# Layer norm of the next tile pair ahead of the last tile's output tail

## The reference

```python
x = x + attention(layernorm(x))     # local window + pooled latents, gated
h = layernorm(x)                    # second phase starts here
for blk in range(3):
    y = qlora_linear(h, 2*blk)      # dequantized 1024x1024 + rank-32 LoRA + bias
    y = gelu(layernorm(y))
    h = qlora_linear(y, 2*blk + 1) + h
x = x + h
```

## Time and profile before

| | us |
|---|---|
| median of 2 runs | 3964.92 (3957.31 to 3972.54) |
| profiled execution, its own time | 3984.25 |
| its span, core 2, the slowest | 3982.6 |
| other cores | 3947.6 to 3982.0 |

### The profile page before, as it was taken

The page is one execution under the profiler, slowest core; times in us unless marked ns, Lnnn a source line. Parts: engine busy times, 40 slices in busy tenths (PEclk is TensorE's granted clock), DMA queues, the critical chain, the costliest instruction groups (busy, mean ns, idle before and its releaser), DMA issues.

```text
span 3982.6 us, 55688 instructions; the slowest of 8 cores (3947.6 to 3982.6 us)
## 1 busy us (share of the span) xinstructions
PE 2472.6 (62%) x19201; PEld 1580.1 (40%) x19216; DVE 1860.7 (47%) x3815; ACT 1122.2 (28%) x1873; POOL 88.5 (2%) x142
## 2 busy tenths in 40 slices
PE   0456665666666566666534857758485766758575
PEld 0344443444433344444302534435253444435343
DVE  0455444545544444554323544545454444545454
ACT  0122333222223322223364323223232322323222
POOL 1000000000000000000021000000000000000000
PEclk9866666776766667666656878879797887978787
DMA  9012111211211111111232020010202001010101
GB/s 143 9 35 33 25 30 30 35 30 29 34 25 30 35 30 30 30 33 25 32 106 68 1 53 1 17 38 1 53 1 53 1 22 33 6 48 1 48 1 33
DMA packets 259700, 128.08 MB, mean 32 GB/s; under 512 B 229232, under 2 KB 233504, under 8 KB 259424
## 3 DMA queue, kind: packets, MB, share of 16 engines
q1 hardware_dynamic: 224512, 62.94, 8.7%
q0 software_dynamic: 34912, 61.57, 7.1%
HBM read 61.99 MB, written 25.17 MB: 22 GB/s over the span
## 4 chain that ended last, share of the span: by engine, by line
PE 46%; DVE 23%; ACT 11%; issue 10%; DMA 4%; another core or an unknown queue 2%; DVEq 2%; SPq 1%; ACTq 1%; POOLq 0%; POOL 0%
PE psA L1292 7%; PE psA L1476 5%; PE psB L1476 5%; PE psB L909 3%; DMA arena<-arena 3%; PE psA L386 3%; PE psA L415 3%; PE psA L778 3%; DVE arena L1419 3%; DVE arena L1413 3%; DVE arena L1399 2%; ACT arena L1433 2%; ACT arena L809 2%; ACT L1380 2%
## 5 line engine op out<-in xcount | busy, mean ns | idle before, releaser
L1292 PE MATMUL psA<-arena,wbig 128*128 128x256 bf16 x3072 | 475.9, 307 | 62.1 <-DVEq L1321 62.0
L1292 PEld LDWEIGHTS psA<-arena,wbig 128*128 128x128 bf16 x3072 | 299.9, 108 | 180.8 <-issue 96.7
L778 PE MATMUL psA<-arena 64*128 64x128 bf16 (+1 forms) x960 | 202.9, 342 | 192.1 <-ACT arena L807 122.5
L1318 DVE TENSOR_SCALAR arena<-psA,biasS 128x256 bf16<-128x256 f32 x384 | 185.8, 484 | 248.8 <-PE psA L1298 199.1
L824 DVE TENSOR_TENSOR arena<-arena,mlocS 128x256 bf16<-128x256 bf16 x480 | 140.4, 292 | 219.2 <-ACT arena L807 104.3
L549 ACT ACT_TABLE_LOAD x16 | 20.5, 1283 | 776.0 <-PE psC L477 776.0
L386 PE MATMUL psA<-wbig,arena 128*128 128x512 bf16 x497 | 139.7, 445 | 135.2 <-DMA arena<-arena 124.0
L1476 PE MATMUL psA<-arena,wbig 128*128 128x256 bf16 x1536 | 223.6, 294 | 0.0
L1476 PE MATMUL psB<-arena,wbig 128*128 128x256 bf16 x1536 | 203.1, 276 | 0.0
L778 PEld LDWEIGHTS psA<-arena 64*128 64x128 bf16 x960 | 75.0, 110 | 306.0 <-issue 293.4
L461 PE MATMUL psA<-arena,wbig 128*128 128x256 bf16 x1024 | 146.9, 312 | 79.5 <-DVEq L509 54.3
(11 more groups left out here) (171 smaller groups left out, 4388.7 us busy)
## 6 DMA issues: line engine op xcount, KB each, us to landing
y<-arena POOLq DMA_DIRECT2D x16, 1024.0 KB, 4.5
arena<-qT POOLq DMA_DIRECT2D x48, 256.0 KB, 2.6
arena<-x_in POOLq DMA_DIRECT2D x16, 512.0 KB, 7.1
x2scr<-arena SPq DMA_DIRECT2D x16, 512.0 KB, 2.9
arena<-x2scr POOLq DMA_DIRECT2D x16, 512.0 KB, 6.5
arena<-arena SPq DMA_TRANSPOSE x224, 3.2
wbig<-wq POOLq DMA_DIRECT2D x1, 2048.0 KB, 18.1
wbig<-wk POOLq DMA_DIRECT2D x1, 2048.0 KB, 29.7
```

The lines of the kernel that those rows point to most:

```text
L778: mm = t.matmul(reg[:, hh * 256 + q0c:hh * 256 + q0c + qn], ar_t.ap()[0:64, o_KR + h * 2 * W + sl * W + koff: o_KR + h * 2 * W + sl * W + ...
L1292: t.matmul(reg, wTv(i0, c, oc * 128, 128), V(hin_o + c * TILE, TILE), start=(c == 0), stop=False)
L1318: v.tensor_scalar(V(y1o + oc * TILE, TILE), Y1REGS[oc % 4], biasS[:, i0 * 8 + oc:i0 * 8 + oc + 1], None, ALU.add)
```

## The change

At the end of a pair, `b_tail(Bst)` is emitted after the layer norm and the transposes of the next A instead of before them. This moves three pieces at once: two transpose issues on SP, two adds on VectorE, and the store of y on POOL. On POOL the store still stands ahead of the load of the next B. Nothing is added or removed.

```diff
                 b_Y2(Bst, k)
                 b_E2(Bst, k)
-            b_tail(Bst)
             if 2 * pair + 2 < nbt_total:
                 emit_ln2(2 * pair + 2)
                 emit_h0(2 * pair + 2)
+            b_tail(Bst)
             if 2 * pair + 3 < nbt_total:
                 emit_x2load(2 * pair + 3)
                 emit_ln2(2 * pair + 3)
```

## The result

The changed kernel takes 4036.2 us (median of 11 runs) beside 3970.2 us of the kernel before (10 runs): ratio 1.0177, interval 1.0143 to 1.0211 (the two medians alone give 1.0166). The forecast was 4037 us and 1.8%. The mean granted clock of the profiled execution's slowest core is 0.753, its own time 4029.6 us and its span 4028.1 us.

A forecast was written before the change was run, and what follows sets the result against it. Pair boundaries were taken as bound by a serial chain of VectorE and DMA. 8.89 us of queue shift plus 1.4 of clock gave 10.29 per boundary, 72.0 in seven, on 3964.92: 4037 us, 1.8% slower; range 4003 to 4062.

The forecast's parts named there:

- TensorE hardly matters at a boundary, two chains end together: At L1298, TensorE's chain and VectorE's norm chain end almost together, TensorE's later by 0 to 0.4 us, mean 0.19.
- A' starts 7.4 us sooner: At a pair boundary, the next A's norm moves ahead of B's tail, so its h0 lands 7.42 us sooner.
- The adds 9.08 us later: B's tail adds wait behind the next A's norm and transposes: start at +13.97 instead of +4.89 us.
- The load uncovered, so the norm of B' moves as much: The next B's x2 load waits for the adds with nothing covering it; that B's norm moves the full 9.08 us.
- L1298 8.89 us later: First matmul needing VectorE's copy L1271, at each boundary: 9.08 less the 0.19 us by which TensorE's chain was later.
- Clock +1.4: After the new idle at a boundary, TensorE restarts at the lower clock: 1.4 us more, bounds 0 and 2.5.
- The rest of the pair stays: The inside of the pairs, between boundaries, keeps its length.
- Rival 2: Added idle raises the granted clock inside pairs, leaving 38 us of added time: 4003 us; chance 0.11.
- Transposes and loads together: At a boundary, slow issues could add 2.3 us, less sharing with loads save 0.5; left out of the sum.
- Rival 1, still more: Boundaries cost more, through slow transpose issues or a longer low-clock start: over 2% slower, 4049 to 4061 us; chance 0.18.
- Rival 4, only the queue shift: At boundaries, clock term 0 and loads 0.5 us quicker: 59 us, 4024; chance 0.67 together with the main case.
- Rival 3, the early start is kept: The next A's h0, 7.42 us sooner, decides the boundary: 52 us gained, 3913 us; chance 0.03.

The follow-up runs named there:

- the kernel before with the load first: Kernel before with one edit: the x2 load of the next B ahead of the tail in POOL's queue; ratio 0.9969 (0.9946 to 0.9991).
- the deferred tail: Against the kernel before: tail transposes first, load behind A's tail, both norms back to back, B's adds and store in the next pair; 0.9878, again 0.9887.
- the filler: Changed kernel plus unused matmuls on TensorE while it waits for L1271; ratio 1.0195 with 96 of them, 1.0188 with 140.

## Why the prediction was right

The added time was foretold as 72.0 us and the path as well. That the number 4037 was met to 1 us is in part luck: the medians lie 66.0 us apart, but the median of the kernel before rose from 3964.92 us (2 runs) to 3970.22 (10 runs). Term by term:

- *TensorE hardly matters at a boundary, two chains end together.* Right: shown by the tie in the kernel before with the load first, and by the deferred tail, where TensorE's chain takes over. The copy's lead over L1298 goes up to 0.67 us (third boundary), so TensorE's chain is later by 0 to 0.5 us, not 0.4; the mean of 0.19 is right.
- *A' starts 7.4 us sooner.* 7.6: L1260 from 19.19 to 11.60. One reading behind it is wrong: the x2 load of A' was not issued in the middle of the pair before. It is emitted there, but POOL runs ahead and issues it one boundary earlier, right behind the load of B' (the L1132 of the earlier trace rows is two loads, x2). The data are there all the same. But three transfers, y's store and two loads, are under way together while VectorE waits for one of them; what the second load costs was not tried.
- *The adds 9.08 us later.* 9.30 (4.92 to 14.22). I had left out the gap of 0.3 us on SP between two batches: four transposes take 5.54 us, not 2 x 2.61.
- *The load uncovered, so the norm of B' moves as much.* 15.40 to 24.41, 9.01 us, with a wait of 7.7 us on average against the 7 to 8 foretold. Shown by moving the load alone. In the changed kernel's two other profiled executions the norm of B' came at +26.13 and +25.30: the load took longer. So on the slowest core this term has a scatter of 1 to 2 us per boundary that one trace of before didn't show; on most of the other cores the norm of B' came at +24.2 to +25.0 in all three.
- *L1298 8.89 us later.* 8.80 (22.65 to 31.45), and 8.88 on cores 4 to 7. L1271 starts at +30.87, where +30.9 was expected.
- *Clock +1.4.* Undersized: 10.86 - 8.82 = 2.04 us, inside its bounds of 0 to 2.5 (1.87 on cores 4 to 7). The stretch took 10.17 to 11.39 us; in the quickest, the first boundary, one output block took 2.12 us and the next 1.89, where 1.19 is the full speed, and a slow part longer than the 3.4 us that I took followed elsewhere. The 0.64 us too little are 4.5 us in seven boundaries. The granted clock was 0.53 in the burst and 0.82 in the stretch after it, and 1.00 in the stretch when the filler ran up to it. The trace agrees with the rule of the Trainium skill (TensorE: Matmul & The Clock Gate, "HAM oscillation — how this bites in real kernels"), that a short burst and a wait leave the next burst slow too; the wait is for VectorE here, where the page has one for a DMA.
- *The rest of the pair stays.* Right: 197.26 us before and 197.31 after on cores 4 to 7. The slowest cores show it 1.13 us shorter after (198.20 to 197.07), but that is core 2 of the kernel before with its longer pairs (granted clock inside them 0.853, on cores 4 to 7 0.857). So 10.8 us per boundary are left, 75.6 in seven, where the prediction had 10.29 and 72.0, and the clock term is the only one that was off by more than 0.3 us. Rival 2 foresaw a clock that gives back 4.8 us per pair; nothing came back, and the deferred tail, with less idle time than the kernel before, has about the same granted clock inside the pairs (0.859 beside 0.857 before and 0.853 after, on cores 4 to 7). Single pairs scatter: 194.2 to 199.1 us on cores 4 to 7 of the kernel before, with the same instructions. The cause of that is open.
- *Transposes and loads together.* The -0.5 us from no longer sharing the DMA engines didn't show: a load at the boundary (both are counted) lands after 6.5 us in the middle after, and 6.6 before. With the tail's transposes first it is 7.3, at most 9.5, but there the h0 transposes and the loads overlap by only 1 to 2 us, as in the kernel before, and the changed kernel run again had loads of up to 9.35 us with no transposes beside them. So no run here shows the rule that the queues take turns (DMA: Bandwidth & Descriptors, "Queues, rings and completion order", in the Trainium skill) at work.
- *Rival 1, still more.* The clock term came in part (+0.5 to +0.6 us beyond the sum). The slow issues did not: each of the four took 1.22 to 1.39 us, and only the gap of 0.3 us between two batches came on top. What the prediction set against it, that issues near the boundaries are all quick, holds for six of the seven: at the fourth boundary of the kernel before one took 2.30 us, beside the slowest load, and A' started at +20.18. The result stayed under the 11.3 us a boundary at which 2% begins.
- *Rival 4, only the queue shift.* Its 4024 us need a clock term of 0, and it was 1.9 to 2.0 us a boundary.
- *Rival 3, the early start is kept.* False as the kernel stands, by the 16.5 us wait at L1298; true as soon as both queues are put right.

## What to carry to other kernels

When a piece of work is moved behind another, follow each of its instructions into its own queue, and ask what hangs on its end in a third queue: here two adds of 2.5 us, moved back on VectorE, took a load on POOL with them, and that load had been covered only by the work that was moved ahead. An engine that starts 7 us sooner has won nothing if the first thing that it needs from its neighbour stands behind all of it. Put the issue of transfers ahead first (the two transposes that need only the last eviction, the load that needs only a free slot), and then move the computing: the same reordering cost 1.8% without this and won 1.0% with it (1.2% with the adds deferred as well).

## What the runs showed that I had not expected

- A filler of matmuls that ends 6.4 us before the real work is no use: the clock had fallen again (10.89 us for the stretch, against 8.52 with the filler up to the work).
- The way from the tail's adds to the norm of B', through store and load on POOL, is no constant: 10.2 us on the slowest core of one profiled execution of the changed kernel, 11.9 and 11.1 in two others, 10.5 before.
- A single core can mislead: core 2 of the kernel before, the slowest, had pairs 0.9 us longer than cores 4 to 7 beside it, and a comparison with it alone gives the change 67.9 us instead of 75.6.
